# A routed expert layer: the list of its tokens made by bfloat16 one-hot products alone, in place of float32 products and scattered writes

## The chip, the cores and the metric

The kernel runs on one core of a Trainium2 chip. The metric is the device time of one execution in microseconds (us), from the first instruction to the last. The engines are TensorE (PE, with its weight loads listed apart as PEld), VectorE (DVE), ScalarE (ACT), GpSimd (POOL) and SyncE (SP), which only issues transfers.

## What is computed

The input is 16 sequences of 1,024 tokens with 256 features. A state-space layer (Mamba) is added to it, then a block with attention over the 16 sequences and a routed expert layer. Of the second part, this is what the change touches:

```
probs = jax.nn.softmax(x @ router_weight, axis=-1)
top_p, top_i = jax.lax.top_k(probs, TOP_K)          # 2 of 8 experts
top_p = top_p / jnp.sum(top_p, -1, keepdims=True)
order = jnp.argsort(top_i.reshape(-1))
within = jnp.arange(N * TOP_K) - offsets[sorted_exp]
keep = within < cap                                 # cap 5120
padded_tokens = zeros.at[slot].set(x[tok_id])       # tokens of each expert, in slots
act = gelu(einsum('ech,ehf->ecf', exp_in, moe_w1))
exp_out = einsum('ecf,efh->ech', act, moe_w2)
moe = zeros.at[padded_ids].add(exp_out * padded_probs[:, None])
```

There are 16,384 tokens and so 32,768 entries (a token with one of its two experts). Each expert's entries are counted, given a rank in the order of the tokens, and put into slots; an expert's slots are rounded up to whole blocks of 256.

## The kernel before

Four stages follow one another, each in a block of its own, so that every engine is done with one before any begins the next: `mamba_stage`, `attention_stage` (which leaves the normalised tokens in `n2` in DRAM, the router's logits in `logits`, and the sum without the experts in `out`), `routing_stage` and `expert_stage`.

**routing_stage** has a head and a list. The head is a chain on DVE over tiles of 128 partitions x 128 tiles x 8 experts (1,024 columns): softmax (its exponential on ACT), the two best experts, with PE making running counts by products with a triangle and with ones, then rank, slot, and whether the entry is kept. DVE waits there on the semaphore `step` after every operation (`after_last`). Then the list: of each slot it needs the token number and the share (the gate). A slot is a pair (lane, column): 128 lanes by `COLS` = 270 columns. The 256 pairs (k, tile), each with 128 entries on the partitions, are shared out:

- `BY_POOL`, 96 of them: POOL writes (token, share) with an indirect DMA to `info` in DRAM, slot by slot.
- `BY_MATMUL`, 160 of them: DVE makes `hot_lane[:, at, z]` (128x128, one-hot in the lane, times the token number for z = 0 and times the share for z = 1) and `hot_column` (128x270, one-hot in the column), and PE adds `hot_lane.T @ hot_column` into `list_bank` in PSUM, for both z, all in float32. The semaphores are `hot` (DVE to PE) and `placed` (PE back to DVE; `HOT_RING` = 4 buffers).

At the end ACT copies `list_bank` to `made`. **expert_stage** loads `info` back as `listing`, adds `made`, makes `token` from it (`e_token`), and then, block by block (135 blocks of 256 slots), gathers the tokens' rows from `n2` (POOL, `gather_rows`), loads the expert's weights (POOL, `load_weights`, row numbers in `weight_row`), transposes, multiplies (`e_ubank`, GELU, `e_ybank`), scales by the share (DVE) and adds the rows to `out` in DRAM (POOL, `add_rows`).

## Time and profile before

| | us |
|---|---|
| three runs | 6548.19, 6549.09, 6552.92; median 6549.09 |
| profiled execution | 6549.9 |
| its span, first to last instruction | 6548.2 |
| mamba and attention stage | up to 4386 |
| routing stage, head | 4386 to 4447 |
| routing stage, list | 4447 to 4596 |
| expert stage | 4596 to the end |

The profiled execution took 1.7 us more than its span. The stages are read from the stretches of the timeline; places in the trace are given in us from the start of the span. Over the whole span PE is busy 94%, POOL 78%, DVE 65%, ACT 54%.

### The profile page before, as it was taken

Reading aid. Unit: us, or ns where it says so; the run is one execution under the profiler, and the core shown is the slowest. Engines: PE = TensorE matmul, PEld = TensorE weight load, DVE = VectorE, ACT = ScalarE, POOL = GpSimd, SP = SyncE. Lnnn points to the kernel's source line nnn. Section 1 sums busy time; section 2 is a strip of 40 time slices with the busy share of each in tenths; the row PEclk is TensorE's granted clock in tenths of the full one; section 3 lists DMA queues with packets and bytes.
Section 4 is the critical chain, followed back from the end, with each engine's and each line's share of the span. In section 5 each row is a group of like instructions: output and inputs, shape, how many; then the busy total and the mean of one; then the engine's idle time right before and its main releaser. Section 6 shows DMA issues by size and latency. Waiting matters only on the chain. (4 is left out here: it accounts for less than half of the span.)

```text
span 6548.2 us, 78761 instructions
## 1 busy us (share of the span) xinstructions
PE 6175.3 (94%) x25444; PEld 3970.3 (61%) x25444; DVE 4267.1 (65%) x5490; ACT 3519.6 (54%) x6418; POOL 5132.0 (78%) x3926
## 2 busy tenths in 40 slices
PE   7999999999999999999998799978999999999999
PEld 3444444444444444444443588866788888888888
DVE  6999999999999999999999377779100000000000
ACT  5677677767676777676766588750222222222222
POOL 6999999999999999999999677736454545454544
PEclk9999999999999999999999999989999999999999
DMA  3555555555555555555555244330566656566554
GB/s 124 166 162 171 166 168 166 168 165 168 165 172 163 166 165 166 170 164 169 166 163 167 62 121 122 116 120 1 175 190 179 190 179 189 180 189 179 183 162 135
DMA packets 551754, 1029.76 MB, mean 157 GB/s; under 512 B 77426, under 2 KB 245876, under 8 KB 516784
## 3 DMA queue, kind: packets, MB, share of 16 engines
q1 hardware_dynamic: 441168, 669.34, 33.3%
q0 software_dynamic: 110176, 355.39, 18.0%
q8 instruction: 204, 3.34, 0.2%
q14 instruction: 206, 1.69, 0.1%
HBM read 926.04 MB, written 88.72 MB: 155 GB/s over the span
## 5 line engine op out<-in xcount | busy, mean ns | idle before, releaser
L361 POOL TENSOR_TENSOR m_dbu<-m_du,m_bb 128x1024 f32<-128x1024 f32 x1024 | 2390.8, 2363 | 0.0
L739 PE MATMUL m_y_bank<-m_prod,m_ident 128*128 128x512 f32 x4096 | 1977.8, 612 | 143.1 <-POOL m_prod L370 143.1
L512 ACT ACTIVATE m_decay<-m_delta,m_a_neg 128x512 f32<-128x512 f32 x2048 | 1419.4, 695 | 724.7 <-DVE m_h L622 722.7
L739 PEld LDWEIGHTS m_y_bank<-m_prod,m_ident 128*128 128x128 f32 x4096 | 789.2, 196 | 1122.9 <-issue 907.2
L1734 DVE TENSOR_SCALAR e_ye<-e_ybank,e_listing 128x256 f32<-128x256 f32 x270 | 118.2, 479 | 1817.1 <-PE e_ybank L1768 1817.1
L622 DVE TENSOR_TENSOR_SCAN m_h<-m_decay,m_h_end,m_dbu 128x512 f32<-128x512 f32 x1024 | 1259.4, 1267 | 3.4 <-ACT m_decay L512 2.5
L622 DVE TENSOR_TENSOR_SCAN m_h<-m_decay,m_dbu 128x512 f32<-128x512 f32 x1024 | 1197.7, 1207 | 13.8 <-ACT m_decay L512 13.2
L1708 ACT ACTIVATE e_a<-e_ubank 128x512 f32<-128x512 f32 x540 | 322.5, 597 | 1473.6 <-PE e_ubank L1759 1473.6
L370 POOL TENSOR_TENSOR m_prod<-m_h,m_cb 128x1024 f32<-128x1024 f32 x416 | 982.5, 2362 | 20.0 <-issue 15.0
L1759 PE MATMUL e_ubank<-e_xT,e_w 128*128 128x256 f32 x4320 | 978.6, 380 | 1.3 <-ACT e_xT L1699 1.3
L1768 PE MATMUL e_ybank<-e_w,e_a 128*128 128x256 f32 x4320 | 954.5, 379 | 0.7 <-ACT e_a L1708 0.7
L1768 PEld LDWEIGHTS e_ybank<-e_w,e_a 128*128 128x128 f32 x4320 | 820.7, 190 | 112.6 <-ACT e_a L1708 1.1
L1651 POOL DMA_INDIRECT e_w<-in_w,weight_row x270 | 258.3, 957 | 799.0 <-PE e_ybank L1768 734.4
L1759 PEld LDWEIGHTS e_ubank<-e_xT,e_w 128*128 128x128 f32 x4320 | 811.6, 190 | 106.7 <-issue 1.6
L604 DVE TENSOR_TENSOR m_prod<-m_h,m_c_bank 128x1024 f32<-128x1024 f32 x608 | 727.3, 1196 | 42.5 <-ACT m_c_bank L499 22.4
L1668 POOL DMA_INDIRECT out<-e_ye,e_token x270 | 429.2, 1590 | 111.0 <-issue 81.3
L706 PE MATMUL m_side<-m_xnT,m_w_in 128*128 128x512 f32 x1024 | 503.0, 600 | 6.0 <-ACT m_xnT L428 6.0
L711 PE MATMUL m_side<-m_xpad,m_tap_diag 128*128 128x512 f32 x1024 | 495.7, 592 | 0.0
L499 ACT COPY m_c_bank<-m_cv 128x512 f32<-128x512 f32 x608 | 359.3, 591 | 95.3 <-DVE m_prod L604 93.1
L706 PEld LDWEIGHTS m_side<-m_xnT,m_w_in 128*128 128x128 f32 x1024 | 198.9, 195 | 260.3 <-issue 258.1
L1659 POOL DMA_INDIRECT e_xe<-n,e_token x270 | 283.8, 1051 | 85.4 <-issue 82.0
L711 PEld LDWEIGHTS m_side<-m_xpad,m_tap_diag 128*128 128x128 f32 x1024 | 194.3, 190 | 245.3 <-issue 245.3
(216 smaller groups left out, 6663.9 us busy)
## 6 DMA issues: line engine op xcount, KB each, us to landing
m_bb<-rows_bc SPq DMA_DIRECT2D x1024, 256.0 KB, 3.8
m_cv<-rows_bc SPq DMA_DIRECT2D x608, 256.0 KB, 4.0
m_cb<-rows_bc SPq DMA_DIRECT2D x416, 256.0 KB, 3.4
m_xin<-in_x SPq DMA_DIRECT2D x32, 512.0 KB, 5.7
m_xres<-in_x SPq DMA_DIRECT2D x32, 512.0 KB, 5.6
x<-m_xres SPq DMA_DIRECT2D x32, 512.0 KB, 6.3
a_xa<-x SPq DMA_DIRECT2D x64, 256.0 KB, 2.9
a_xr<-x SPq DMA_DIRECT2D x64, 256.0 KB, 3.2
```

Source lines behind the costliest of these rows:

```text
L361: nc.gpsimd.tensor_tensor(dbu[:, slot], du[:, q[1], p * PC:(p + 1) * PC], bb[:, slot].unsqueeze(1).to_broadcast([P, PC, T]), ALU.mult).the ...
L370: nc.gpsimd.tensor_tensor(prod[:, slot], h[:, slot], cb[:, C_BUFFER[k]].unsqueeze(1).to_broadcast([P, PC, T]), ALU.mult).then_inc(prod_by_ ...
L499: nc.scalar.copy(c_bank[:], cv[:, V_BUFFER[k]]).then_inc(c_copied, 1)
L512: nc.scalar.activation(decay[:, cc], delta[:, r, c], ACT.Exp, scale=a_neg[:, c, n:n + 1]).then_inc(decay_done, 1)
L604: nc.vector.tensor_tensor(prod[:, slot], h[:, slot], c_bank[:].unsqueeze(1).to_broadcast([P, PC, T]), ALU.mult).then_inc(prod_by_vector, 1)
L622: nc.vector.tensor_tensor_scan(h[:, slot, cc], decay[:, cc], dbu[:, slot, cc], h_end[:, u, cc:cc + 1] if r else 0.0, ALU.mult, ALU.add).th ...
L706: ins = nc.tensor.matmul(bank, w_in[:, piece, col:col + P], xnT[:, piece], start=(piece == 0), stop=final)
L711: ins = nc.tensor.matmul(bank, tap_diag[:, i, piece], xpad[:, i, piece:piece + T], start=(piece == 0), stop=final)
L739: ins = nc.tensor.matmul(y_bank[:, cc], ident[:], prod[:, slot, cc], start=False, stop=(n == NS - 1))
L1668: nc.gpsimd.indirect_dma_start(out, bass.IndirectOffsetOnAxis(ap=token[:, col:col + 1], axis=0), ye[:, n % Y_RING, j], None, compute_op=AL ...
L1759: ins = nc.tensor.matmul(ubank[:, (n * UG + g) % U_RING, i], w1[:, r, k, c * P:(c + 1) * P], xT[:, n % 2, k], start=(k == 0), stop=(k == K ...
L1768: ins = nc.tensor.matmul(ybank[:, n % 2, j], a[:, n % 2, c, j * P:(j + 1) * P], w2[:, n % W_RING, c], start=(c == 0), stop=(c == FC - 1))
```

## The change

Lists. All 256 pairs (k, tile) go by products now; the scattered writes, `info`, its clearing and its reading back, and `made` are gone. The pairs are taken in 32 groups of 8 (`SPAN` = 4 tiles, k innermost). For each group DVE makes one `hot_lane` of 128 lanes x 8 entries in bfloat16 (`EACH` = 8, the entries innermost in memory, so that one entry's 128 lanes lie 16 bytes apart) by one tensor_tensor, ACT makes `hot_row` from it (times the partition number), and the eight `hot_column` (128x270 bfloat16, times tile + 1) are made by DVE in even groups and by POOL in odd ones. PE multiplies each entry's `hot_row` and `hot_lane` with its `hot_column`, 512 products. Token numbers come out as partition + 128 x tile, small enough parts for bfloat16.

Shares. They no longer go through the list. They are written to DRAM behind each token's row: `n2` gets 260 columns (`ROW`) in place of 256, the last four being two shares and two marks of the expert. The expert stage gathers them with the row, and DVE picks the share by two small operations for each block.

Order. The identity, the buffers of the gathered rows, the norm vectors and the weights of the first two blocks are prepared in the routing stage (`Shared`, `load_expert`); the block table (`passed_e` to `weight_row`) is made within the list, after group 4; the token numbers are finished on DVE at the end of the routing stage.

```diff
@@ routing_stage, constants and tiles
-    SCATTERS_OPEN = 16
-    BY_POOL, BY_MATMUL = ENTRIES[0::8] + ENTRIES[3::8] + ENTRIES[6::8], [
-        e for j in (1, 2, 4, 5, 7) for e in ENTRIES[j::8]]
+    SPAN = 4
+    EACH = SPAN * TOPK
+    GROUPS = TILES // SPAN
     HOT_RING = 4
+    BY_POOL = [g for g in range(GROUPS) if g % 2]
+    BY_VECTOR = [g for g in range(GROUPS) if g not in BY_POOL]
+    WEIGHTS_AT = 4
-        hot_lane = sb("hot_lane", [P, HOT_RING, 2, P])
-        hot_column = sb("hot_column", [P, HOT_RING, COLS])
+        hot_lane = sb("hot_lane", [P, HOT_RING, P, EACH], BF16)
+        hot_row = sb("hot_row", [P, HOT_RING, P, EACH], BF16)
+        hot_column = sb("hot_column", [P, HOT_RING, EACH, COLS], BF16)
+        def columns(eng, g, made):
+            at = g % HOT_RING
+            for j in range(EACH):
+                tile, k = g * SPAN + j // TOPK, j % TOPK
+                ins = eng.tensor_scalar(hot_column[:, at, j], column_h[:], column_of[:, tile, k:k + 1], float(tile + 1),
+                                        ALU.is_equal, ALU.mult)
+            ins.then_inc(made, 1)
@@ SyncE
+            sp.wait_ge(gates_made, 2)
+            sp.dma_start(n2[:, H:ROW].rearrange("(t p) z -> p t z", p=P),
+                         gate[:].rearrange("p t z k -> p t (z k)")).then_inc(gates_stored, 16)
+            sp.wait_ge(gates_stored, 16)
@@ GpSimd
-            for n, (k, tile) in enumerate(BY_POOL):
-                ...
-                nc.gpsimd.indirect_dma_start(
-                    info, bass.IndirectOffsetOnAxis(ap=slot_of[:, k, tile:tile + 1], axis=0),
-                    entry[:, k, tile], None, bounds_check=P * COLS - 1, oob_is_err=False).then_inc(scattered[turn % 2], 16)
+            pool.wait_ge(located, 1)
+            for g in BY_POOL:
+                wait(pool, placed, g - HOT_RING + 1)
+                columns(nc.gpsimd, g, column_by_pool)
+                if g == BY_POOL[-2]:
+                    pool.wait_ge(rows_made, 1)
+                    load_expert(nc, w, shared, 0)
+            load_expert(nc, w, shared, 1)
@@ ScalarE
-            nc.scalar.copy(made[:].rearrange("p c z -> p z c"), list_bank[:, :, 0:COLS])
+            for g in range(GROUPS):
+                act.wait_ge(lane_made, g + 1)
+                wait(act, placed, g - HOT_RING + 1)
+                nc.scalar.activation(hot_row[:, g % HOT_RING], hot_lane[:, g % HOT_RING], ACT.Identity,
+                                     scale=row_f[:]).then_inc(row_made, 1)
@@ TensorE
-            for n in range(len(BY_MATMUL)):
-                pe.wait_ge(hot, n + 1)
-                for z in range(2):
-                    ins = nc.tensor.matmul(list_bank[:, z, 0:COLS], hot_lane[:, n % HOT_RING, z], hot_column[:, n % HOT_RING],
-                                           start=(n == 0), stop=(n == len(BY_MATMUL) - 1))
+            for g in range(GROUPS):
+                ...
+                for j in range(EACH):
+                    for z, of in enumerate((hot_row, hot_lane)):
+                        ins = nc.tensor.matmul(list_bank[:, z, 0:COLS], of[:, at, :, j], hot_column[:, at, j],
+                                               start=(g == 0 and j == 0), stop=(g == GROUPS - 1 and j == EACH - 1))
                 ins.then_inc(placed, 1)
@@ VectorE
-            for n, (k, tile) in enumerate(BY_MATMUL):
-                wait(dve, placed, n - HOT_RING + 1)
-                at = n % HOT_RING
-                for z in range(2):
-                    nc.vector.tensor_scalar(hot_lane[:, at, z], lane_f[:], place[:, k, tile:tile + 1], entry[:, k, tile, z:z + 1],
-                                            ALU.is_equal, ALU.mult)
-                nc.vector.tensor_scalar(hot_column[:, at], column_f[:], column[:, k, tile:tile + 1], None,
-                                        ALU.is_equal).then_inc(hot, 1)
+            for g in range(GROUPS):
+                ...
+                wait(dve, placed, g - HOT_RING + 1)
+                tt(hot_lane[:, at], lane_h[:],
+                   lane_of_h[:, tiles].rearrange("p t k -> p (t k)").unsqueeze(1).to_broadcast([P, P, EACH]),
+                   ALU.is_equal).then_inc(lane_made, 1)
+                if g in BY_VECTOR:
+                    columns(nc.vector, g, column_by_vector)
+                if g == WEIGHTS_AT:
+                    ...
+            dve.wait_ge(all_placed, 1)
+            after_last(nc.vector.tensor_scalar(whole[:], list_bank[:, 1, 0:COLS], 1.0, None, ALU.max))
+            after_last(nc.vector.reciprocal(whole[:], whole[:]))
+            after_last(tt(whole[:], whole[:], list_bank[:, 0, 0:COLS], ALU.mult))
+            ...
+            nc.vector.tensor_copy(shared.token[:], whole[:])
@@ expert_stage
+                nc.vector.scalar_tensor_tensor(out=match[:, n % 2], in0=rows[:, :, H + TOPK:ROW], scalar=shared.mark_of[:, n:n + 1],
+                                               in1=rows[:, :, H:H + TOPK], op0=ALU.is_equal,
+                                               op1=ALU.mult).then_inc(weighted, 1)
+                ...
+                nc.vector.reduce_sum(share[:, n % 2], match[:, n % 2], axis=AXX).then_inc(weighted, 1)
```

In the program of DVE, at the end of the head, from the operation after the rank is complete (`r_best` and `r_rank` are the one-hot choice and the slot, `r_kept` whether it is kept), this stood before:

```order
L1560 TENSOR_TENSOR r_prob<-r_best,r_work 128x1024
L1561 TENSOR_REDUCE r_kept<-r_prob 128x128
L1562 TENSOR_TENSOR r_prob<-r_best,r_rank 128x1024
L1563 TENSOR_REDUCE r_slot_f<-r_prob 128x128
L1560 TENSOR_TENSOR r_prob<-r_best,r_work 128x1024
L1561 TENSOR_REDUCE r_kept<-r_prob 128x128
L1562 TENSOR_TENSOR r_prob<-r_best,r_rank 128x1024
L1563 TENSOR_REDUCE r_slot_f<-r_prob 128x128
```

and at the same place stands now:

```order
L1617 TENSOR_TENSOR r_rank<-r_rank,r_work 128x1024
L1619 TENSOR_TENSOR r_prob<-r_best,r_rank 128x1024
L1620 TENSOR_REDUCE r_slot_f<-r_prob 128x128
L1619 TENSOR_TENSOR r_prob<-r_best,r_rank 128x1024
L1620 TENSOR_REDUCE r_slot_f<-r_prob 128x128
```

Four operations over 1,024 columns are gone there and one is new. Where the list begins, DVE now has this, with the block table (`r_passed_e` to `s_weight_row`) behind the columns of group 4:

```order
L1626 TENSOR_SCALAR r_column_of<-r_column_of 128x256
L1633 TENSOR_TENSOR r_hot_lane<-r_lane_h,r_lane_of_h 128x1024
L1470 TENSOR_SCALAR r_hot_column<-r_column_h,r_column_of 128x270 x8
L1633 TENSOR_TENSOR r_hot_lane<-r_lane_h,r_lane_of_h 128x1024 x2
L1470 TENSOR_SCALAR r_hot_column<-r_column_h,r_column_of 128x270 x8
L1633 TENSOR_TENSOR r_hot_lane<-r_lane_h,r_lane_of_h 128x1024 x2
L1470 TENSOR_SCALAR r_hot_column<-r_column_h,r_column_of 128x270 x8
L1639 TENSOR_TENSOR r_passed_e<-r_blocks_to,r_block_f 128x1080
L1641 TENSOR_REDUCE r_expert_f<-r_passed_e 128x135
```

Before, two `r_hot_lane` and one `r_hot_column` stood there for each of 160 pairs, with the block table ahead of them. In the program of POOL, from the last of the constants on, this stood before (the scatters, then the expert stage):

```order
L1447 AFFINE_SELECT r_earlier<-r_earlier 128x128
L1456 DMA info<-r_entry,r_slot_of 34560x2 x96
L1645 UNCONDITIONAL_BRANCH
L1651 DMA e_w<-in_w,weight_row 128x2048 x2
L1673 IOTA e_dump_i 128x2
L1674 MEMSET e_xe 128x1536
L1675 MEMSET e_ident 128x128
L1677 AFFINE_SELECT e_ident<-e_ident 128x128
L1659 DMA e_xe<-n,e_token 128x256 x2
```

and now:

```order
L1495 MEMSET s_ident 128x128
L1496 MEMSET s_xe 128x1560
L1498 AFFINE_SELECT r_earlier<-r_earlier 128x128
L1500 AFFINE_SELECT s_ident<-s_ident 128x128
L1470 TENSOR_SCALAR r_hot_column<-r_column_h,r_column_of 128x270 x120
```

The constants of the expert stage have moved ahead of the list, and 128 tensor_scalar (these 120 and 8 more behind the first expert's weight load) stand where 96 scatters stood.

## Rows read from the trace of the kernel before

**Rows 1.** Windows; us, busy by engine, PEclk, DMA share, GB/s.

```profile
4386.00:4447.00 61.00, 5.06 (x8) 1.99 (x8) 50.63 (x75) 1.06 (x1) 4.79 (x21) 0.56 0.04 13
4447.00:4596.00 149.00, 148.18 (x640) 122.76 (x640) 140.92 (x480) 0.03 (x1) 99.49 (x94) 0.98 0.02 1
...
4612.00:6548.00 1936.00, 1926.22 (x9176) 1695.01 (x9176) 118.22 (x270) 446.16 (x810) 964.35 (x803) 1.00 0.59 178
```

**Rows 2.** Timeline from the list's end to the expert stage's first transpose.

```profile
4595.97 0.63 ACT L1467 COPY made<-r_list_bank 128x540 f32<-128x540 f32 x1 [199.93 <-PEq L1487]
...
4604.34 0.30 DVE L1728 CAST e_token<-e_token_f 128x270 int32<-128x270 f32 x1
4605.42 1.05 POOL L1659 DMA_INDIRECT e_xe<-n,e_token  x1 [3.45 <-DVE e_token L1728]
...
4609.81 1.09 PE L1746 MATMUL e_tbank<-e_ident,e_xe 128*128 128x128 f32 x4 [13.97 <-DMA e_xe<-n,e_token]
```

**Rows 3.** Groups by line in the list (busy us, mean ns, idle before).

```profile
L1483 PE MATMUL r_list_bank<-r_hot_column,r_hot_lane 128*128 128x270 f32 x640 | 148.2, 395 | 27.4 <-DVE r_hot_column L1591 27.4
L1483 PEld LDWEIGHTS r_list_bank<-r_hot_column,r_hot_lane 128*128 128x128 f32 x640 | 122.8, 192 | 53.2 <-DVE r_hot_column L1591 28.3
L1589 DVE TENSOR_SCALAR r_hot_lane<-r_lane_f,r_place,r_entry 128x128 f32<-128x128 f32 x320 | 102.5, 364 | 5.2 <-PE r_list_bank L1483 1.1
L1456 POOL DMA_INDIRECT info<-r_entry,r_slot_of x96 | 101.8, 1061 | 83.9 <-DVE r_slot_of L1577 54.9 <-issue 28.9
L1591 DVE TENSOR_SCALAR r_hot_column<-r_column_f,r_column 128x270 f32<-128x270 f32 x160 | 61.5, 385 | 0.0
```

**Rows 4.** Timeline of DVE where the list begins.

```profile
4446.74 0.60 DVE L1589 TENSOR_SCALAR r_hot_lane<-r_lane_f,r_place,r_entry 128x128 f32<-128x128 f32 x2
4447.25 0.36 DVE L1591 TENSOR_SCALAR r_hot_column<-r_column_f,r_column 128x270 f32<-128x270 f32 x1
4447.52 0.60 DVE L1589 TENSOR_SCALAR r_hot_lane<-r_lane_f,r_place,r_entry 128x128 f32<-128x128 f32 x2
```

**Rows 5.** Timeline of DVE in the head.

```profile
4415.07 0.95 DVE L1539 RECIPROCAL r_line<-r_line 128x128 f32<-128x128 f32 x1
...
4427.03 0.69 DVE L1557 TENSOR_SCALAR r_work<-r_rank 128x1024 f32<-128x1024 f32 x1
...
4434.04 1.23 DVE L1560 TENSOR_TENSOR r_prob<-r_best,r_work 128x1024 f32<-128x1024 f32 x1
...
4439.07 0.29 DVE L1564 CAST r_slot_of<-r_slot_f 128x256 int32<-128x256 f32 x1
...
4443.08 1.27 DVE L1578 TENSOR_TENSOR r_passed_e<-r_blocks_to,r_block_f 128x1080 f32<-128x1080 f32 x1
```

**Rows 6.** POOL's elementwise work: one from the timeline, one group of the page.

```profile
4388.83 0.29 POOL L1447 TENSOR_SCALAR_AFFINE_SELECT r_earlier<-r_earlier 128x128 f32<-128x128 f32 x1
...
L361 POOL TENSOR_TENSOR m_dbu<-m_du,m_bb 128x1024 f32<-128x1024 f32 x1024 | 2390.8, 2363 | 0.0
```

**Rows 7.** Attention stage: DVE beside POOL in the timeline, and L1217's durations (min/median/max).

```profile
3907.77 1.46 DVE L1217 TENSOR_SCALAR a_n<-a_hid,a_moments,a_rs 128x256 f32<-128x256 f32 x2
3907.02 0.71 POOL L1022 TENSOR_TENSOR a_rs<-a_rs,a_minus_half 128x2 f32<-128x2 f32 x1
...
3908.14 1.13 POOL L1007 TENSOR_TENSOR a_rs<-a_tmp,a_minus_half 128x2 f32<-128x2 f32 x1
...
L1217 DVE TENSOR_SCALAR a_n<-a_hid,a_moments,a_rs x128: 315/754/1339, 3801.5 to 4379.5; 128x256 f32<-128x256 f32 x128
```

**Rows 8.** TensorE: a strided weight load and a bfloat16 product (durations), and one timeline row.

```profile
L1324 PEld LDWEIGHTS a_side<-a_w_proj,a_oT x512: 291/309/337, 3784.4 to 4371.7; 128*128 128x128 f32 x171
...
4203.91 2.05 PE L1324 MATMUL a_side<-a_w_proj,a_oT 128*128 128x256 f32 x8
...
L1261 PE MATMUL a_score<-a_causal,a_rows_of x256: 384/384/386, 3697.2 to 4314.3; 16*32 16x512 bf16 x128
```

**Rows 9.** DMA issues: KB each, median us to landing.

```profile
m_w_x<-in_x_T SPq DMA_DIRECT2D x2, 32.0 KB, 2.9
```

More of the change, by code:

```diff
@@ L1505, in _ @@
             tt = nc.vector.tensor_tensor
-            dve.wait_ge(const, CONST + 1)
-            after_last(nc.vector.tensor_copy(row_f[:], row_i[:]))
-            after_last(nc.vector.tensor_copy(lane_f[:], lane_i[:]))
-            after_last(nc.vector.tensor_copy(column_f[:], column_i[:]))
-            after_last(nc.vector.memset(place[:], 0.0))
-            for k in range(TOPK):
-                after_last(nc.vector.tensor_copy(entry[:, k, :, 0], token_i[:]))
-            after_last(nc.vector.tensor_copy(block_f[:], block_i[:]))
-            after_last(nc.vector.tensor_copy(step_f[:], step_i[:]))
-            after_last(nc.vector.memset(kept[:], 0.0))
             dve.wait_ge(loaded, 16)
@@ L1556, in _ @@
             after_last(tt(rank[:], rank[:], within[:], ALU.add))
-            after_last(nc.vector.tensor_scalar(work[:], rank[:], float(CAP), None, ALU.is_lt))
+            after_last(nc.vector.tensor_scalar(work[:], rank[:], float(CAP), NOWHERE, ALU.is_ge, ALU.mult))
             after_last(tt(rank[:], rank[:], per_expert(first_slot[:]), ALU.add))
+            after_last(tt(rank[:], rank[:], work[:], ALU.add))
             for k in range(TOPK):
-                after_last(tt(prob[:], best[k][:], work[:], ALU.mult))
-                after_last(nc.vector.reduce_sum(kept[:, k], prob[:], axis=AXX))
@@ L1569, in _ @@
-            after_last(nc.vector.scalar_tensor_tensor(out=slot_f[:], in0=place[:], scalar=float(COLS), in1=column[:],
-                                                      op0=ALU.mult, op1=ALU.add))
-            after_last(nc.vector.scalar_tensor_tensor(out=column[:], in0=column[:], scalar=1.0, in1=kept[:],
-                                                      op0=ALU.add, op1=ALU.mult))
-            after_last(nc.vector.tensor_scalar(column[:], column[:], -1.0, None, ALU.add))
-            after_last(nc.vector.scalar_tensor_tensor(out=slot_f[:], in0=slot_f[:], scalar=float(-P * COLS), in1=kept[:],
-                                                      op0=ALU.add, op1=ALU.mult))
@@ new lines, in _, with expert_stage @@
+            after_last(nc.vector.scalar_tensor_tensor(out=vacant[:], in0=list_bank[:, 1, 0:COLS], scalar=0.0, in1=dump_f[:],
+                                                      op0=ALU.is_equal, op1=ALU.mult))
+            after_last(nc.vector.scalar_tensor_tensor(out=whole[:], in0=whole[:], scalar=0.25 - P, in1=vacant[:],
+                                                      op0=ALU.add, op1=ALU.add))
+            nc.vector.tensor_copy(shared.token[:], whole[:])
+def expert_stage(nc, w, n2, shared, out):
@@ L1622, in expert_stage @@
         ybank = al.ps("ybank", [P, 2, J, H])
[L1623 to L1627 removed]
+        weighted = sem("weighted")
         x_loaded = [sem("x_loaded%d" % r) for r in range(X_RING)]
```

234 lines of the change are left out of this document (116 added, 118 removed).

## The prediction

> **What bounds the kernel now.** I read the windows first. The reader is to see three stretches [rows 1]. In the expert stage, PE is busy 1,926 of 1,936 us at full clock with the DMA engines at 0.59: nothing the change adds there on DVE, POOL or the queues is on the path unless it reaches PE. In the head, DVE is busy 50.6 of 61 us and the others nearly idle: a chain on DVE. In the list, PE is busy 148.2 of 149 us, DVE 140.9, POOL 99.5. DVE's figure misleads: the timeline at the start of the list, before PE pushes back, shows one entry (two lane operations and a column) from 4446.74 to 4447.52, 0.78 us [rows 4], so 160 entries would be 125 us; the other 24 are waits for `placed`. PE's 640 records (two for each float32 product) take 148.2 / 640 = 0.2316 us each [rows 3]. So PE sets the pace of the list, and POOL's 96 scatters (101.8 us, [rows 3]) lie beneath it and are worth nothing by themselves. The list counts from DVE's first lane operation, 4446.74 [rows 4], to where ACT's copy begins, 4595.97 [rows 2]: 149.2 us. From there to the first transpose of the expert stage, 4609.81 [rows 2], are 13.8 us in which PE stands still.
>
> **The head, up to the first lane operation.** Six casts now stand where DVE had waited for the exponential: 2.1 us (one over 1,024 columns at 0.70, the others at 0.30 down to 0.15, from the sizes of [rows 5]) against a wait of 1.2 us (ACT's 1.06 us [rows 1] and the hand-over): +0.9. The reciprocal, 0.95 us [rows 5], now comes before PE may start its counts, where it ran beneath them: +1.0. One more tensor_tensor over 1,024 columns: +1.25. Four operations of that size gone: 4 x 1.26 [rows 5] = -5.0. Before, from 4439.07 [rows 5] to 4446.74 [rows 4] went the eleven operations over 256 columns and the block table, 7.7 us; now six of them, 2.1 us: -5.6. The sum is **-7.5 us**. The block table (3.9 us with its new operation) moves into the list. The longer constants on POOL (some 5 us from 4386) end before DVE needs them, because DVE does the load and the maximum first.
>
> **The list, engine by engine.**
> - PE: 512 bfloat16 products of 270 columns. A bfloat16 product of 512 columns lasts 384 ns [rows 8], as long as a float32 record of 270 columns, 395 ns [rows 3]; so I scale the pace: 0.2316 x 270 / 512 = 0.122 us, 62.5 us in all. Upper bound: no faster than a float32 record, 119 us.
> - DVE: 32 lane operations. If bfloat16 lets tensor_tensor take two elements a step, as tensor_scalar does in float32 (0.69 us over 1,024 columns, [rows 5]), one costs 0.69 less the overlap of 0.08 (two of 0.34 in 0.60, [rows 4]): 0.61, 19.5 us. Bound: 1.23 each [rows 5], 39 us. I take the first. 128 columns: a float32 one costs 0.27 [rows 4]; I take 0.26, 33.3 us. With the block table: **56.7 us**.
> - POOL: 128 columns of 270. No row has this operation. The nearest is the affine_select, 0.29 us over 128 columns [rows 6], some 0.1 of it fixed: 0.50 over 270, 0.45 with overlap, **57.6 us**. Lower bound: as on DVE, 0.26, 33 us. Upper: the two-input rate, 2.363 us for 1,024 [rows 6], 0.75 for 270 with the fixed part, 96 us.
> - ACT: 32 operations of 1,024 columns at 1.06 [rows 1], 34 us, hidden while PE or DVE sets the pace.
>
> Now what they do to each other. In the attention stage two tensor_scalar of 256 columns on DVE, 315 ns each at best, last 1.46 us beside POOL, and POOL's power operation, 0.71 alone, lasts 1.13; their ends fall together [rows 7]. The median of that DVE operation is 754 ns [rows 7]. So DVE's tensor_scalar from SBUF to SBUF and POOL's elementwise work take turns. In the old list POOL only issued transfers. In the new one both stream columns all the time, so I add them: 56.7 + 57.6 = 114.3, plus 1.9 for PE's last group: **116 us**, where PE needs only 62.5. Gain 149.2 - 116 = 33.2. Lower end, POOL at 0.26: 92 us. Upper, with a hand-over of 0.15 (1.13 less 0.71 less 0.29, [rows 7]) at each of POOL's 128: 135 us.
>
> Rows 7 show this only for tensor_scalar. For the lane operations, two tensors from SBUF, no row tells; if they run beside POOL, 19.5 us come off and the kernel takes 6486. The Trainium skill (SBUF — State Buffer, Who interferes with whom) says that DVE with two SBUF inputs also contends with a GpSimd operation that reads SBUF, and that the loser blocks for the whole instruction; by it they don't.
>
> **The end of the list.** Seven DVE operations over 270 columns now follow the products: the reciprocal at 0.95 x 270 / 128 = 2.0 [rows 5], four with two operands at 0.45 or less (between the 0.29 and 1.23 of [rows 5]), two at 0.3: 4.5 us. Then the stage's boundary, 0.25, and from the finished token numbers to the first transpose 5.17 us as before (4604.64 to 4609.81, [rows 2]): 9.9 in place of 13.8, **-3.9 us**. The weights are there already.
>
> **At nothing.** The shares' store has 16,384 pieces of 16 bytes. 512 pieces land in 2.9 us [rows 9]; 32 times that, 93 us, is the bound, from 4418 to 4511, under a list that ends at 4555; if the list were short it could cost 5 us. Rows of 1,040 bytes: 16 more for each of 34,560 gathers are 0.55 MB, 3 us at 178 GB/s [rows 1], beneath PE. The two small operations a block on DVE (118 of 1,936 us busy, [rows 1]) lie beneath PE too. In the attention stage the tokens' stores get a pitch of 1,040 bytes; I put 0 to +4 us there and take 0.
>
> **Sum.** 7.5 + 33.2 + 3.9 = 44.6 us less than the profiled execution's 6549.9 (which is 0.8 over the median of the three runs): **6505 us**. The likeliest case's own range is 6483 to 6530.
>
> **Rivals.**
> 1. *DVE and POOL don't hinder each other here.* For it: DVE's lane operations ran at their pace beside POOL's scatters [rows 3]. Against it: rows 7. Then PE is the bound: 62.5, 2.7 for the first group and some 2 for a start at half clock (0.56 granted in the head, [rows 1]): 67 us. Gain 7.5 + 82.2 + 3.9: 6456 us.
> 2. *PE's weight loads from entries 16 bytes apart.* A strided load (128 bytes apart, float32) lasted 309 ns [rows 8] against 192 packed [rows 3], and eight such records took 2.05 us, 0.256 each [rows 8]. Behind a product of 0.122 us a load can't hide as it did behind one of 0.23. At 0.256 PE needs 131 us, with the start 134: gain 26.6, 6523 us. Against it: those loads were of 4-byte elements at eight times the distance. It decides from 0.22 us a product. The Trainium skill says both things: SBUF — State Buffer (Door 1) that 16-byte lines want at least two hits each, which would bring 6523; TensorE: Matmul & The Clock Gate (Fast Weight Load) that 128 non-float32 columns load faster, packed or strided, which would leave the 62.5. No row settles it.
> 3. *POOL's tensor_scalar is slow and takes turns: slower than before.* At the two-input rate with hand-over, 0.90 us each, the list takes 56.7 + 115 + 1.9 = 174 us, 24 more, less 11.4: 6562 us. It breaks even when a POOL column costs (149.2 + 11.4 - 56.7 - 1.9) / 128 = 0.80 us. For it: nothing in the trace shows POOL at one input of bfloat16 with a scalar; against it: the affine_select.
> 4. *The change trades one full list for another and nothing is left*: costs near 0.80: within 0.2%.
>
> **Chances.** Taking turns as summed, 0.53; rival 1, 0.24; rival 2, 0.14; rival 3, 0.06; rival 4, 0.03. A measurement of this kernel tells about 0.2% (13 us) from no change. Faster by more: 0.53 + 0.24 + 0.14 = 0.91; within: 0.03; slower: 0.06. The range, 6450 to 6532, holds the first three but for their tails.
>
> **What would show it.** In the profile after: PE well under full in the list, DVE's column operations longer than 0.4 us and POOL's unequal in length where both are busy: turns. PE full with products 0.12 us apart: rival 1; PE full at 0.2 or more: rival 2. The first lane operation should start near 4439, the expert stage's first transpose 9.9 us after the last product, and each block of the expert stage should be as long as before. The prediction is wrong if POOL's column alone is far from 0.45 us.

## The result and the profile after

The changed kernel takes 6565.45 us (median of 14 runs, 6562.13 to 6568.48) against 6550.59 for the kernel before (14 runs): 1.0023 times as long, 95% interval 1.0015 to 1.0031. It is slower, by just over what can be told from no change, where 44.6 us less were forecast. Its profiled execution took 6567.1 us, its span 6565.4.

Windows of the changed kernel, in the columns of [rows 1]; they are cut at the first lane operation, the end of the products, the first transpose of the expert stage and the end of its last product:

```profile
4390.00:4441.00 51.00, 6.04 (x8) 2.35 (x8) 42.11 (x58) 1.06 (x1) 3.45 (x16) 0.53 0.70 9
4441.00:4611.00 170.00, 93.48 (x512) 73.53 (x512) 58.70 (x167) 36.65 (x32) 163.85 (x132) 0.74 0.05 17
4611.00:4621.00 10.00, 0.00 (x0) 0.00 (x0) 3.91 (x7) 0.00 (x0) 3.16 (x4) 0.62 0.46 172
4621.00:6550.00 1929.00, 1926.96 (x9180) 1696.17 (x9180) 156.10 (x538) 446.70 (x811) 962.24 (x801) 1.00 0.60 178
6550.00:6565.00 15.00, 0.04 (x1) 0.00 (x0) 0.88 (x2) 0.00 (x0) 3.12 (x2) 0.57 0.15 17
```

In the list it is now POOL that is hardly ever idle (163.9 of 170 us); PE has gone from 148 of 149 us to 93 of 170, DVE from 141 to 59. The timeline of POOL and of DVE, from the first lane operation on and (POOL) at the end of the list:

```profile
4440.66 35.42 POOL L1470 TENSOR_SCALAR r_hot_column<-r_column_h,r_column_of 128x270 bf16<-128x270 bf16 x25 [47.47 <-DVEq L1627]
...
4597.36 9.53 POOL L1470 TENSOR_SCALAR r_hot_column<-r_column_h,r_column_of 128x270 bf16<-128x270 bf16 x8
...
4440.65 0.69 DVE L1633 TENSOR_TENSOR r_hot_lane<-r_lane_h,r_lane_of_h 128x1024 bf16<-128x1024 bf16 x1
4441.26 2.09 DVE L1470 TENSOR_SCALAR r_hot_column<-r_column_h,r_column_of 128x270 bf16<-128x270 bf16 x8
4443.27 1.28 DVE L1633 TENSOR_TENSOR r_hot_lane<-r_lane_h,r_lane_of_h 128x1024 bf16<-128x1024 bf16 x2
...
4468.41 0.95 DVE L1633 TENSOR_TENSOR r_hot_lane<-r_lane_h,r_lane_of_h 128x1024 bf16<-128x1024 bf16 x1 [6.94 <-PE r_list_bank L1544]
```

A POOL column takes 1.42 us in the first stretch, in which DVE works beside it for part of the time (25 in 35.42), and 1.19 in the last group, when DVE rests (8 in 9.53). Within the first stretch, while DVE is silent, three columns take 3.74 us and start 1.27 us apart; why they are not 1.19 apart there, no run shows. A DVE column takes 0.25 (8 from 4441.26 to 4443.27). So DVE is soon four groups ahead and waits. What the two do to each other is plainest where one of DVE's lane operations meets a POOL column (single rows, the first with DVE silent):

```profile
4464.53 3.74 POOL L1470 TENSOR_SCALAR r_hot_column<-r_column_h,r_column_of 128x270 bf16<-128x270 bf16 x3
...
4458.81 1.75 POOL L1470 TENSOR_SCALAR r_hot_column<-r_column_h,r_column_of 128x270 bf16<-128x270 bf16 x1
4458.85 0.69 DVE L1633 TENSOR_TENSOR r_hot_lane<-r_lane_h,r_lane_of_h 128x1024 bf16<-128x1024 bf16 x1 [1.18 <-PE r_list_bank L1544]
...
4468.34 1.20 POOL L1470 TENSOR_SCALAR r_hot_column<-r_column_h,r_column_of 128x270 bf16<-128x270 bf16 x1
```

In the first meeting the POOL column is stretched to 1.75 us and the lane operation keeps its 0.69. In the second (DVE's row at 4468.41, shown above) the column keeps its 1.20 and the lane operation is stretched to 0.95. Of the 32 lane operations 12 last 0.71 to 0.99 us; with all columns on DVE (e1, below) none lasts over 0.69.

The waits in the list say who paces whom; columns are us in all, times, longest:

```profile
DVE r_hot_lane L1633 <- PE r_list_bank L1544: 89.5, 28, 6.9
PE r_list_bank L1544 <- POOL r_hot_column L1470: 73.5, 16, 6.3
PE r_list_bank L1544 <- DVE r_hot_column L1470: 20.0, 1, 20.0
```

Where the time went, in the two profiled executions (the span grew by 17.2 us; the forecast was -44.6):

| stretch | before | after | difference | forecast |
|---|---|---|---|---|
| up to routing's first transfer | 4386.6 | 4387.3 | +0.7 | 0 |
| head, from there to the first lane operation | 60.2 | 53.4 | -6.8 | -7.5 |
| list, to the operation that reads the products | 149.2 | 169.9 | +20.7 | -33.2 |
| from there to the first transpose | 13.8 | 10.5 | -3.3 | -3.9 |
| expert stage, to the end of its last product | 1929.3 | 1928.9 | -0.3 | 0 |
| behind the last product | 9.1 | 15.3 | +6.2 | 0 |

The last row was in nobody's sum. This is the last run of products of the changed kernel, which ends at 6550.03, and POOL's last transfer; nothing follows in the timeline up to 6565.4:

```profile
6542.86 7.17 PE L1796 MATMUL e_ybank<-s_w,e_a 128*128 128x256 f32 x32 [0.69 <-ACT e_a L1744]
6553.15 1.56 POOL L1713 DMA_INDIRECT out<-e_ye,s_token  x1 [0.30 <-issue]
```

The views leave out instructions that only synchronise. The raw records of the trace have them: behind the landing of the last added rows POOL runs a drain, of 1.84 us in the kernel before and of 7.97 us in the changed one, and with it the program ends.

### The profile page after: what moved, and what is told of

The parts are those of the page before. It is cut to its first block and busy times, and to the rows that moved or that the text cites. A ratio compares the mean times of both kernels' runs of the same rounds, so it can differ in the third digit from the quotient of the medians.

```text
span 6565.4 us, 78602 instructions
## 1 busy us (share of the span) xinstructions
PE 6120.1 (93%) x25316; PEld 3921.9 (60%) x25316; DVE 4215.0 (64%) x5430; ACT 3554.0 (54%) x6449; POOL 5192.8 (79%) x3956
## 3 DMA queue, kind: packets, MB, share of 16 engines
q1 hardware_dynamic: 457280, 669.05, 33.2%
q14 instruction: 206, 1.69, 0.1%
## 5 line engine op out<-in xcount | busy, mean ns | idle before, releaser
L1763 DVE TENSOR_SCALAR e_ye<-e_ybank,e_share 128x256 f32<-128x256 f32 x270 | 118.2, 479 | 1768.3 <-PE e_ybank L1796 1768.3
L1787 PE MATMUL e_ubank<-e_xT,s_w 128*128 128x256 f32 x4320 | 978.4, 380 | 1.3 <-ACT e_xT L1735 1.3
L1796 PE MATMUL e_ybank<-s_w,e_a 128*128 128x256 f32 x4320 | 954.5, 379 | 0.7 <-ACT e_a L1744 0.7
L1796 PEld LDWEIGHTS e_ybank<-s_w,e_a 128*128 128x128 f32 x4320 | 821.0, 190 | 112.4 <-ACT e_a L1744 1.1
L1787 PEld LDWEIGHTS e_ubank<-e_xT,s_w 128*128 128x128 f32 x4320 | 811.7, 190 | 106.5 <-issue 1.6
L1384 POOL DMA_INDIRECT s_w<-in_w,s_weight_row x270 | 259.7, 962 | 776.9 <-PE e_ybank L1796 735.1
L1713 POOL DMA_INDIRECT out<-e_ye,s_token x270 | 430.4, 1594 | 111.1 <-issue 81.4
L1704 POOL DMA_INDIRECT s_xe<-n,s_token x270 | 282.5, 1046 | 89.9 <-issue 82.3
```

What stands on the lines that cost most here:

```text
L1713: nc.gpsimd.indirect_dma_start(out, bass.IndirectOffsetOnAxis(ap=token[:, col:col + 1], axis=0), ye[:, n % Y_RING, j], None, compute_op=AL ...
L1787: ins = nc.tensor.matmul(ubank[:, (n * UG + g) % U_RING, i], w1[:, r, k, c * P:(c + 1) * P], xT[:, n % 2, k], start=(k == 0), stop=(k == K ...
L1796: ins = nc.tensor.matmul(ybank[:, n % 2, j], a[:, n % 2, c, j * P:(j + 1) * P], w2[:, n % W_RING, c], start=(c == 0), stop=(c == FC - 1))
```

## The experiments

All of them change the changed kernel. "All on VectorE" is the base of most. Times are of one execution unless runs are named. In these kernels the two stages ahead of routing end anywhere from 4382.0 to 4391.2 us, though nothing in them was changed, so single executions are better compared by their list: from the first lane operation to the operation that reads the products.

**All columns on VectorE** (e1):

```diff
-    BY_POOL = [g for g in range(GROUPS) if g % 2]
+    BY_POOL = []
```

> All 256 hot columns are made by VectorE, none by GpSimd, which only loads the weights. Theory (GpSimd's own 1.19 us for a column set the list's pace of 170 us): the list is now VectorE's, 32 lane operations of 0.6 us, 256 columns of 0.25 us and 3.9 us of block table, 87 to 92 us, so 6483 to 6492 us in all, and lane operations come back from 0.69 to about 0.61 us. Rival, TensorE's half clock: a group's 16 products take 3.6 us at the 0.225 us of the half clock, so if the clock stays down the list is TensorE's at 115 us, 6510 in all. Rival, the strided weights cost something beyond the clock: likewise over 110 us.

6474.42 us (5 runs, 6470.28 to 6474.63), against 6565.45 for the changed kernel, and 6568.26 where it was run again (c2, 4 runs): 91 to 94 us less. The list takes 76.7 us, less than expected. DVE's timeline where it begins:

```profile
4440.84 0.69 DVE L1628 TENSOR_TENSOR r_hot_lane<-r_lane_h,r_lane_of_h 128x1024 bf16<-128x1024 bf16 x1
4441.45 1.69 DVE L1470 TENSOR_SCALAR r_hot_column<-r_column_h,r_column_of 128x270 bf16<-128x270 bf16 x8
4443.06 0.68 DVE L1628 TENSOR_TENSOR r_hot_lane<-r_lane_h,r_lane_of_h 128x1024 bf16<-128x1024 bf16 x1
```

Without POOL beside it a column costs 0.20 us (1.61 for eight) and a lane operation 0.60. 32 x 0.60 + 256 x 0.20 + 3.6 for the block table + 2.3 for PE's last group are 76.3 of the 76.7 us. The window of its list, in the columns of [rows 1]:

```profile
4441.00:4518.00 77.00, 67.93 (x512) 61.15 (x512) 74.49 (x295) 36.85 (x32) 4.71 (x4) 0.92 0.15 56
```

DVE sets the pace, PE is close behind with 512 products, 0.118 us apart where the clock is full, as it is for most of the list (0.92 granted). The half-clock rival is out.

**All columns on GpSimd** (e2), `BY_POOL = list(range(GROUPS))`:

> All 256 hot columns are made by GpSimd; VectorE makes only the lanes and the block table. Theory (a GpSimd column costs 1.19 us by itself): 32 groups of 9.5 to 9.6 us, a list of 305 to 310 us, 6700 us in all. Rival (a GpSimd column costs 0.45 us and the two engines hinder each other): with VectorE nearly silent 256 columns take 115 to 150 us, 6510 to 6545 us in all.

6711.27 us, a list of 317.6. With DVE all but silent:

```profile
L1470 POOL TENSOR_SCALAR r_hot_column<-r_column_h,r_column_of 128x270 bf16<-128x270 bf16 x256 | 305.4, 1209 | 52.9 <-DVEq L1627 47.3
```

256 columns in 305.4 us are 1.19 each: the 1.19 us are POOL's own.

**Six groups on GpSimd** (e3), `BY_POOL = [4, 9, 14, 19, 24, 29]`, `HOT_RING = 8`:

> Six of the 32 groups of columns on GpSimd instead of sixteen, and rings of eight groups instead of four, so that VectorE can run ahead of them. Theory (GpSimd's own pace, the little hindrance as measured): GpSimd is busy 6 x 9.6 to 12 = 58 to 72 us and hidden; VectorE has 32 x 0.65 + 208 x 0.27 + 3.9 = 81 us, so 6476 to 6482 us in all, some 6 to 10 us less than with all columns on VectorE. Rival (the engines take turns): VectorE's 81 and GpSimd's 58 add up to 139 us, 6535 us in all. Rival: the end of the list waits for the last GpSimd group, no gain over all on VectorE.

6473.73 us (5 runs), the same as with none, where 6 to 10 us less were expected; the list takes 77.4. POOL did work alongside, but DVE's eight columns then took 1.86 to 2.18 us instead of 1.69:

```profile
4438.18 2.09 DVE L1470 TENSOR_SCALAR r_hot_column<-r_column_h,r_column_of 128x270 bf16<-128x270 bf16 x8
...
4443.34 1.86 DVE L1470 TENSOR_SCALAR r_hot_column<-r_column_h,r_column_of 128x270 bf16<-128x270 bf16 x8
```

Six groups taken off DVE save 6 x 1.61 = 9.7 us, and some 0.2 to 0.5 us more on each of the other groups while POOL works, with some stretched lane operations, give it back. The turns theory (139 us) fails as well.

**GpSimd reads float32** (e4):

```diff
+            number = column_f if g in BY_POOL else column_h
-                ins = eng.tensor_scalar(hot_column[:, at, j], column_h[:], ...
+                ins = eng.tensor_scalar(hot_column[:, at, j], number[:], ...
```

> As the changed kernel, but GpSimd's columns read float32 column numbers and still write bfloat16. Theory A (the cost is GpSimd's two-operation form with a scalar from memory, whatever the type): 1.19 us stays, no change in time. Theory B (reading bfloat16 is what is slow): columns fall to between 0.5 and 0.8 us, the list to 90 to 120 us.

6567.4 us, and 1.29 us a column against 1.28 (128 in the time from the first to the last, without the weight transfers between them): the type does not matter.

**The forms by themselves** (e6), behind the last added row, one of the eight as an example:

```diff
+            for j in range(8):
+                ins = eng.tensor_scalar(f_out[:, j], f_in[:], f_s[:, j:j + 1], 2.0, ALU.is_equal, ALU.mult)
```

> As all columns on VectorE, and behind the last added row eight operations each of eight forms, first on GpSimd and then on VectorE with nothing beside them; their output is not used. On GpSimd the column's form (is_equal with a scalar from memory, then mult) is expected at 1.19 us alone. Theory A (the cost is in the two-operation form or the scalar from memory): without the second operation, or with immediate scalars, under 0.7 us. Theory B (a comparison is what is slow): add and mult with a scalar from memory under 0.7 us. Theory C (it is the element rate, 270 elements at some 4 ns): all forms of tensor_scalar 1.1 to 1.3 us and half the width 0.6 us. On VectorE the column's form 0.20 us in bfloat16 and about 0.3 us in float32.

POOL's groups, mean ns of one behind the bar (L1701 the column's form, L1713 the same in float32, L1707 immediate scalars, L1704 is_equal alone, L1716 half the width, L1720 tensor_tensor subtract, L1710 add and mult):

```profile
L1701 POOL TENSOR_SCALAR e_f_out<-e_f_in,e_f_s 128x270 bf16<-128x270 bf16 x8 | 9.5, 1194 | 0.1
L1713 POOL TENSOR_SCALAR e_f_out<-e_f_in,e_f_s 128x270 f32<-128x270 f32 x8 | 9.4, 1198 | 0.1
L1707 POOL TENSOR_SCALAR e_f_out<-e_f_in 128x270 bf16<-128x270 bf16 x8 | 8.7, 1123 | 0.1
L1704 POOL TENSOR_SCALAR e_f_out<-e_f_in,e_f_s 128x270 bf16<-128x270 bf16 x8 | 7.5, 959 | 0.1
L1716 POOL TENSOR_SCALAR e_f_out<-e_f_in,e_f_s 128x135 bf16<-128x135 bf16 x8 | 5.9, 760 | 0.1
L1720 POOL TENSOR_TENSOR e_f_out<-e_f_in,e_f_sh 128x270 bf16<-128x270 bf16 x8 | 4.8, 633 | 0.1
L1710 POOL TENSOR_SCALAR e_f_out<-e_f_in,e_f_s 128x270 bf16<-128x270 bf16 x8 | 3.8, 489 | 0.1
```

Half the width saves 434 ns, so 3.2 ns an element and 0.33 us fixed. Of the two-operation forms only add+mult was cheap, which looked like theory B. DVE does the column's form in 0.20 us (8 in 1.69), in float32 0.27 (8 in 2.26).

**GpSimd with subtract and mult** (e9), `ALU.subtract if g in BY_POOL else ALU.is_equal`. The list then holds no valid entries; the expert stage takes a fixed list of tokens instead, so only the list's time counts:

> The changed kernel with GpSimd's columns made by subtract and mult instead of is_equal and mult; the list then holds no valid entries, so the token list is replaced by a fixed one, and only the list's time counts. GpSimd's form cost 0.49 us by itself in the run of the forms, near the 0.45 us of the prediction. If the price of the comparison is all that failed, the prediction's sum returns. Its turns: VectorE 54 us and GpSimd 63 us one after the other and the hand-overs, 115 to 125 us from the first lane to the end of the list instead of 170. Rival (the two engines work side by side and only slow each other by a quarter): 16 GpSimd groups of 4 to 5 us beside VectorE, 75 to 90 us.

Neither: 1.29 us a column and a list of 171.2. Theory B falls: leaving out the comparison does not help by itself.

**The forms again** (e12), POOL alone:

> As the run of the forms, on GpSimd alone, with other forms of tensor_scalar over 270 bfloat16 numbers with a scalar from memory, eight times each: add+mult, subtract+mult, mult+add, mult+mult, add+add, then add, subtract, mult and max alone. If only pairs that GpSimd has a fast path for are cheap, add+mult is again 0.49 us and subtract+mult 1.19 us. Theory: any pair with subtract, a comparison or max is slow, and those of add and mult are fast. Rival: the 0.49 us came from the numbers used (all ones and a factor of two) and add+mult takes 1.19 us with a factor of three.

add+mult 0.49, mult+add 0.50, mult+mult 0.49; subtract+mult 1.20, add+add 1.22; add, subtract, mult, max alone 0.96 to 0.97. Four of its groups (L1701 add+mult, L1704 subtract+mult, L1713 add+add, L1716 add alone); durations in ns are least, median and longest:

```profile
L1701 POOL TENSOR_SCALAR e_f_out<-e_f_in,e_f_s x8: 490/491/502, 6463.5 to 6466.8; 128x270 bf16<-128x270 bf16 x8
L1704 POOL TENSOR_SCALAR e_f_out<-e_f_in,e_f_s x8: 1197/1197/1236, 6467.4 to 6475.7; 128x270 bf16<-128x270 bf16 x8
L1713 POOL TENSOR_SCALAR e_f_out<-e_f_in,e_f_s x8: 1209/1212/1238, 6484.8 to 6493.2; 128x270 bf16<-128x270 bf16 x8
L1716 POOL TENSOR_SCALAR e_f_out<-e_f_in,e_f_s x8: 967/971/974, 6494.5 to 6501.1; 128x270 bf16<-128x270 bf16 x8
```

So three pairs are cheap, add+mult with other numbers too; a single operation costs twice as much as those pairs. My theory of "add and mult" was too wide: add+add and mult alone are slow.

**GpSimd with add and mult** (e10), near the prediction's own price at last (0.49 us for 0.45), again with a list that isn't valid and a fixed list of tokens:

```diff
-                                        ALU.is_equal, ALU.mult)
+                                        ALU.add if g in BY_POOL else ALU.is_equal, ALU.mult)
```

> As the last kernel with arithmetic columns on GpSimd, but with add and mult, the one two-operation form that took 0.49 us in the run of the forms; subtract and mult took 1.27 us in the list, so the price hangs on the pair of operations, not on there being a comparison. The list's entries are again invalid and the token list a fixed one; only the list's time counts. The prediction's turns at its price: 54 us of VectorE and 63 of GpSimd one after the other, 115 to 125 us from the first lane to the end of the list. Rival (side by side, each slowed by about a quarter as seen in the changed kernel): 16 groups of 4 to 5 us on GpSimd beside 62 us on VectorE, 75 to 90 us.

6483.71 us, a list of 89.8. In its timeline, POOL's columns are 0.73 us apart instead of 0.49 (44 in 32.18) and DVE's there 0.32 to 0.33 instead of 0.20, later up to 0.43:

```profile
4437.92 32.18 POOL L1471 TENSOR_SCALAR r_hot_column<-r_column_h,r_column_of 128x270 bf16<-128x270 bf16 x44
...
4440.75 2.64 DVE L1471 TENSOR_SCALAR r_hot_column<-r_column_h,r_column_of 128x270 bf16<-128x270 bf16 x8
```

Had the columns taken turns, the shares of time at which each keeps its own pace (0.49 / 0.73 = 0.67 and 0.20 / 0.33 = 0.61) would add up to 1; they add up to 1.3. In the changed kernel they add up to 1.19 / 1.42 + 0.20 / 0.25 = 1.6. So the engines do hinder each other, well short of turns. And even at this price the list with POOL's help is 13 us longer than DVE's alone. POOL still sets the pace there: its 128 columns take 84.8 of the 89.8 us, 0.66 each. A smaller share for POOL at this price was not run.

**Entries outermost** (e7), all on VectorE:

```diff
-        hot_lane = sb("hot_lane", [P, HOT_RING, P, EACH], BF16)
+        hot_lane = sb("hot_lane", [P, HOT_RING, EACH, P], BF16)
-                        ins = nc.tensor.matmul(list_bank[:, z, 0:COLS], of[:, at, :, j], hot_column[:, at, j],
+                        ins = nc.tensor.matmul(list_bank[:, z, 0:COLS], of[:, at, j], hot_column[:, at, j],
```

> As all columns on VectorE, but the hot lanes are laid out with the entries outermost, so that VectorE reads the lane of each entry with a stride of zero and TensorE reads its weights side by side. Theory (the stride of the weights costs TensorE nothing, the layout pays on VectorE): a lane operation rises from 0.68 to 1.1 to 1.2 us by the 2.41 us of the 2,160 elements in the run of the forms, VectorE still bounds the list, which goes from 77 to 92 to 95 us; the product's step stays at 0.116 us. Rival (strided weights cost something): the product's step falls below 0.116 us or weight loads below 0.14 us.

6485.57 us, a list of 93.6. A lane operation takes 1.21 us instead of 0.69. A weight load of an entry, with its lanes 16 bytes apart (e1) and side by side (e7):

```profile
L1539 PEld LDWEIGHTS r_list_bank<-r_hot_column,r_hot_lane x256: 141/144/173, 4443.3 to 4517.1; 128*128 128x128 bf16 x128
L1539 PEld LDWEIGHTS r_list_bank<-r_hot_column,r_hot_lane x256: 95/98/152, 4438.4 to 4528.5; 128*128 128x128 bf16 x128
```

So the strided load does last longer, 0.144 us against 0.098, as the rival had it. But it lies beside the products, which are 0.118 us apart with it and 0.116 without. The layout pays on DVE (17 us) and costs PE 0.002 us a product, hidden in this list.

**The kernel before and the changed kernel once more** (c1, c2):

> The kernel before, again, on this chip, for its trace. The runs of before beside the first four experiments took 6660.66 us where earlier ones took 6550.59, while the changed kernel's timing did not move. Theory: the 110 us lie in what only the kernel before has, the scatters of entries into the list in memory by GpSimd, so the stretch of the list is 260 us instead of 149 and all others are as before. Rival: they lie in an earlier stage (mamba or attention) and the kernels of the change do not have them by luck of placement. If this chip gives 6550 us, nothing is told.

> The changed kernel as it is. If only the kernel before depends on the chip, this takes 6562 to 6569 us whatever the kernel before takes; if the chip is slower for both, it takes some 6675 us where the kernel before takes 6660.

The kernel before took 6661.0 us here, 111 more, and all of it in the list; the changed kernel 6568.26, unmoved. The window inside the list of the kernel before, and one entry of DVE's:

```profile
4480.00:4560.00 80.00, 16.15 (x31) 8.43 (x29) 6.45 (x21) 0.00 (x0) 60.96 (x63) 0.50 0.02 1
...
4499.58 0.85 DVE L1589 TENSOR_SCALAR r_hot_lane<-r_lane_f,r_place,r_entry 128x128 f32<-128x128 f32 x2 [10.37 <-remote]
```

While POOL issues scatters, PE stands still for some 9 us and DVE for some 10 of 11.2 us an entry, and the clock falls to half (0.50 granted); once the scatters are over they run at their old pace. Beside the experiments up to e12 the kernel before took 6661 to 6663 us, beside e13 to e16 and in the result 6550; why, stays open. Chip 5 gave 6662 us beside e10 and 6550 beside e15, so the chip alone does not decide it. The ratio at the top holds where it is undisturbed; where it is not, the changed kernel, which has no scatters, is faster: 0.986 (0.9845 to 0.9875).

**The late end.** Five edits of "all on VectorE", each judged by the time behind the last product: ln_vecs loaded by SyncE in the expert stage (e5); fillers meant to bring each engine's count of instructions to that of the kernel before, modulo 256 (e8; in the traces VectorE's and ScalarE's counts do match so, the others' don't quite); `ROW = H`, no shares stored or looked up (e11); 96 or 48 more indirect transfers on POOL's queue (e13, e14); the identity made by POOL in the expert stage (e15). The core of two of them, e11 and e15:

```diff
-ROW = H + 2 * TOPK
+ROW = H
-            sp.dma_start(n2[:, H:ROW].rearrange("(t p) z -> p t z", p=P), ...
```

```diff
             gather_rows(0)
+            nc.gpsimd.memset(ident[:], 0.0).then_inc(ident_made, 1)
+            ...
             gather_rows(1)
```

> As all columns on VectorE (6474 us), and the load of ln_vecs issued by SyncE in the expert stage, as before the change, so that SyncE has a block of its own in the last stage. In the changed kernel the span ends 8.8 us after the last packet of the added rows, in the kernel before 2.1 us. Theory (a SyncE that has no work in the last stage makes the end of the program late): last packet to end falls back to 2 to 3 us, 6468 us in all. Rival (the end of the program is late for another reason, the number of semaphores or of instructions): 8.8 us stay, 6474 us.

> As all columns on VectorE, with filler instructions (increments of an unused semaphore while the engines wait at the start of routing) so that each engine's count of instructions before the end of the program stands as in the kernel before, modulo 256. Theory (the late end of the program, 8.8 us behind the last packet instead of 2.1, hangs on where the last instructions lie in what is loaded): the end falls back to 2 to 3 us. Rival (it hangs on something else): 8 to 9 us stay.

> As all columns on VectorE, with the rows of n2 back at 256 numbers without the shares, so no shares are stored or loaded, the expert stage's VectorE has no look-up of the share (a share of one half stands for all), and GpSimd no wait for it. Theory (the late end of the program comes with the wider rows or the two operations a block that read them): the end falls from 15.3 to 9 us behind the last product, 6467 us in all. Rival (it comes with the rest of the new structure): 15.3 us stay. In either case the pitch of a block of the expert stage stays 14.25 us.

> As all columns on VectorE, with 96 more indirect transfers on GpSimd's queue in the routing stage (each a gather of 128 rows of logits into an unused tile), as many as the scatters that the change took out. The records of the trace put the 6.2 us at the end into one instruction, GpSimd's drain behind its last transfer: 1.84 us in the kernel before, 7.97 us in every kernel of the change, which issues 810 indirect transfers where the kernel before issues 906. Theory (the drain's length hangs on how many transfers the queue has issued by then): with 906 again the drain is 1.84 us and the program ends 9.1 us behind the last product. Rival (it hangs on something else of the new structure): 7.97 us and 15.3 us stay. The extra transfers delay the routing stage by themselves, so only the end counts.

> As the one with 96 more indirect transfers, with 48. If the drain at the end grows or shrinks step by step with the number issued, it lies between 1.84 and 7.97 us; if it has two values, it is one of them; if the number doesn't matter, 7.97 us.

> As all columns on VectorE, with the identity for the transposes made by GpSimd in the expert stage, behind the first gathers, so that GpSimd again has operations of its own in that stage, as in the kernel before. Theory (the drain of 7.97 us comes of a last stage in which GpSimd only issues transfers): it falls to 1.84 us, the end to 9.1 us behind the last product, and the time by some 6 us to 6466 us. Rival (it does not hang on that): 7.97 us stay, no change.

They took 6473.72 us (e5, 5 runs), 6481.94 (e8; its fillers make the head 66.4 us long instead of 53.6), 6471.2 (e11), 6495.75 (e13; the transfers delay the weights), 6471.77 (e14) and 6473.35 (e15, 4 runs). POOL's last drain, from the raw records, and the time from the end of the last product to the end of the span:

```
kernel                                drain us   behind the last product us
before, and before again (c1)         1.84       9.1, 9.1
changed, and changed again (c2)       7.97       15.3, 15.3
all on VectorE (e1, e16)              7.97       15.3, 15.1
e5, e8, e11, e13, e14, e15            7.97       15.2 to 15.4
```

None moved it. In e6 and e12, where GpSimd computes for 54 us and more behind the last added row, the drain lasts 7.97 us as well. What is shown is where the 6.2 us are (6.13 of them in the drain) and that none of these edits removes them; their cause stays open.

**The better version** is all on VectorE, run again beside e15:

> All columns on VectorE once more, beside the kernel with the identity made late, and beside the kernel before on this chip. 6468 to 6475 us again, whether the kernel before takes 6550 or 6660 us.

6474.19 us (4 runs) where the kernel before took 6549.99 (7 runs) on the same chip, 0.9881 (0.9865 to 0.9898).

## Why the prediction was wrong

- **POOL's column, the step that failed.** "No row has this operation. The nearest is the affine_select": 0.45 us, at most 0.75, against 1.19 by itself (e2, e6) and 1.28 in the list. The upper bound came from another operation, with two tensors at 2.3 ns an element [rows 6], and so did not bound anything; is_equal+mult costs 3.2 ns an element. Even so, that bound was not carried into the sum: at 0.75 us by turns the list is 56.7 + 96 + 1.9 = 154.6 us and the kernel takes 6544, outside the range that was given. As it ran, 128 columns took 154.09 + 9.53 = 163.6 us of the list's 169.9; the rest is 2.6 us for POOL's weight transfers between its groups and 3.7 from its last column to the operation that reads the products, with PE's last group in it, mostly at half clock.
- **Rival 3 hit the number by luck.** It gave a list of 174 us and 6562 us, 0.06 likely, from 0.90 us a column and turns. It came out at 169.9 and 6565, from 1.28 us a column and no turns: POOL bounds the list alone. That POOL's tensor_scalar is slow was its right half, and with no row for the operation 0.06 was too little for that. The break-even of 0.80 us was worked out with turns too. From the measured terms it is, as an estimate, (149.2 + 10.1 - 6.3) / 128 = 1.20 us a column in the list (10.1 for the head and the end of the list, 6.3 for what is not POOL's columns), or 1.15 with the 6.2 us at the program's end.
- **Taking turns.** Wrong in the strict form on which the sum rested. At the forecast price the sum said 116 us and e10 measured 89.8. So two errors stood against each other: the turns made the forecast 26 us too long, the price 80 too short (169.9 - 89.8). The hand-over in the upper end is mis-sized by a little: 1.13 - 0.71 - 0.29 is 0.13, not 0.15. [Rows 7] showed two engines whose ends fell together once, which is hindrance, but not how much. Nearest to turns come the lane operations, which the prediction set apart for want of a row: in each meeting shown above one of the two is stretched, the POOL column by 0.55 us or the lane operation by 0.26. The Trainium skill (SBUF — State Buffer, Who interferes with whom) says that a VectorE operation in a two-port mode, or one with two SBUF inputs beside a GpSimd operation that reads SBUF, and the GpSimd operation lock each other out: whichever starts first keeps the other waiting for its whole instruction. Here DVE made a column each 0.25 us while POOL's lasted 1.42, and a lane operation that started 0.07 us behind a POOL column was done some 0.2 us before it, so the trace does not agree. Which mode DVE's columns ran in, no run shows.
- **DVE.** Lane operation forecast 0.61, measured 0.60 where POOL leaves it alone; block table 3.9, measured 3.6 to 3.9. Right. Column 0.26, measured 0.20 alone, so too high as a price of its own, and 0.25 beside POOL.
- **PE.** Product forecast 0.122 us, measured 0.118 at full clock and 0.225 at half (1.2 of 2.4 GHz). Rival 2, the strided weights, is out: they load more slowly, but not so that the products wait (e7). What the sum left out is that PE, idle for 4.6 us before each POOL group on average (73.5 in 16 waits), falls to half clock (0.74 granted in the list): sixteen products at 0.225 are 3.6 us, 3.4 in the last group. It costs only behind POOL's last group.
- **Rival 1**, no hindrance, 6456 us: its list of 67 us, bound by PE, was not reached by any run; 76.7 is the nearest, where POOL makes no columns.
- **The head**, -7.5, measured -6.8. **The end of the list**, -3.9, measured -3.3, because the first gather follows 6.35 us behind the start of the first operation on the sums where with all on VectorE it is 5.55 (POOL comes late from its own last transfers: its drain behind them ends at 4615.94 by the raw records, 0.8 us behind DVE's). Both right within 0.7.
- **At nothing.** The shares' store landed 25.0 us after its issue, where 93 was the bound. The wider rows, that store and the two small operations a block cost nothing that can be told: the expert stage is 0.3 us shorter up to its last product, and e11, without them, gains 3 us in all, which is inside the scatter of these kernels. Right.
- **What no step named**: the 6.2 us in POOL's last drain. Without them the result would be 0.1% slower, that is, no change; with all columns on DVE they are the only stretch that is longer than in the kernel before.

## What to carry to other kernels

A price for an operation that no row shows is not bounded by rows of other operations on the same engine: on POOL the pair of operations alone moved the price by 2.4 times. Before work is shared out to a second engine, work out the price from which it sets the pace, and when nothing bounds the price below that, give the bad case its full weight. And a second engine's help has to pay for what it takes from the first: here six groups moved to POOL gave nothing. Sixteen at its best price lost 13 us, because half of the work was still too much for it.

## What the runs showed of the hardware

- GpSimd's tensor_scalar over 128 x 270 bfloat16: add+mult, mult+add and mult+mult 0.49 us; add, subtract, mult, max or is_equal alone 0.96; is_equal+mult, subtract+mult and add+add 1.19 to 1.22. VectorE does is_equal+mult and add+mult in 0.20 (8 in 1.69 and 8 in 1.70, with the end of the last). The Trainium skill (GPSIMD Engine Reference, Engine selection) has one-input work on GpSimd at roughly line rate; the runs do not agree, for the two forms tried on both engines take 2.4 and 6 times as long on GpSimd as on VectorE.
- VectorE and GpSimd side by side slow each other by a fifth to two thirds (0.20 to 0.25 and 1.19 to 1.42; 0.20 to 0.33 and 0.49 to 0.73), short of turns. A bfloat16 tensor_tensor on VectorE with two inputs in SBUF either stretches the GpSimd column beside it (1.20 to 1.75 us) or is stretched by it (0.69 to 0.95); 12 of 32 lasted 0.71 to 0.99.
- bfloat16 weights whose elements lie 16 bytes apart load in 0.144 us, packed ones in 0.098; products of 270 columns then follow each other 0.118 and 0.116 us apart.
- In some runs GpSimd's scatters held up PE and DVE by 9 to 10 us an entry; in others the same kernel ran undisturbed. And GpSimd's drain at the end of the program lasted 1.84 us in both profiled executions of the kernel before and 7.97 in all of the changed kernel and its variants.
